# Cross-attention stage: inverse roots on POOL, unscaled exponentials, another order of PE's products

## The reference, cut to what matters

```python
x = x + attn(_layernorm(x), qkv_w, qkv_b, proj_w, proj_b)   # projection and residual end here
q = _layernorm(x)
kp = k @ Wk.T ; vp = v @ Wv.T + bv ; qp = q @ Wq.T + bq      # k = v = ctx, 77 rows a batch
scores = (qp @ kp.T) / sqrt(256)
x = x + (softmax(scores) @ vp) @ Wo.T + bo
xn = rmsnorm(_layernorm(x)) * norm_weight
logits = xn @ router_w.T + router_b ; probs = softmax(logits)
```

## Time and profile before

| what | us |
|---|---|
| median of three runs | 1166.14 (1165.2 to 1168.48) |
| profiled execution | 1170.64 |
| its span | 1168.9 |
| PE busy | 1066.8 (91%) |
| DVE busy | 1009.0 (86%) |
| ACT busy | 767.8 (66%) |
| POOL busy | 533.4 (46%) |
| the stage, first projection to last gates | 772.84 to 895.67 |

### The profile page before, as it was taken

How to read it: one execution, slowest core, us unless ns; L and a number is a source line. 1 busy time by engine, 2 the same in 40 slices (tenths; PEclk the granted TensorE clock), 3 DMA queues, 4 the chain that set the end, 5 groups by cost and what they waited for, 6 DMA issues and landing times. The chain is left out here.

```text
span 1168.9 us, 23162 instructions
## 1 busy us (share of the span) xinstructions
PE 1066.8 (91%) x8508; PEld 593.9 (51%) x8508; DVE 1009.0 (86%) x2108; ACT 767.8 (66%) x932; POOL 533.4 (46%) x866
## 2 busy tenths in 40 slices
PE   7988899999999999999999999988883069999998
PEld 6875433333333333333333333357773048888897
DVE  8998999999999999999999999437998975666653
ACT  4551288888888888888888888944555024555653
POOL 2647945454545363545444523232200023766665
PEclk8998599999999999999999999989997559999999
DMA  6787743232322334242424220055522022554443
GB/s 236 260 250 216 173 80 80 49 74 50 77 56 63 62 64 70 46 78 50 84 39 85 48 54 16 21 153 175 191 84 95 0 87 70 145 144 115 113 113 36
DMA packets 90140, 114.03 MB, mean 98 GB/s; under 512 B 31104, under 2 KB 62832, under 8 KB 90032
## 3 DMA queue, kind: packets, MB, share of 16 engines
q1 hardware_dynamic: 66872, 69.57, 20.5%
q0 software_dynamic: 19824, 36.48, 15.8%
q10 hardware_dynamic: 3336, 6.56, 1.6%
HBM read 73.31 MB, written 38.27 MB: 95 GB/s over the span
## 5 line engine op out<-in xcount | busy, mean ns | idle before, releaser
L835 DVE TENSOR_REDUCE b_max_halves<-banks 128x1 f32<-128x512 f32 x1024 | 625.1, 681 | 7.5 <-PE banks L882 7.5
L760 ACT ACTIVATE b_probs<-banks 128x1024 f32<-128x1024 f32 x512 | 520.4, 1027 | 110.8 <-PE banks L913 110.8
L882 PE MATMUL banks<-b_k,b_q 62*128 62x512 f32 x1024 | 391.9, 467 | 12.3 <-DVE b_max_halves L835 4.5
L913 PE MATMUL banks<-b_q,b_k 64*128 64x512 f32 x1024 | 378.8, 453 | 0.1
L898 PE MATMUL banks<-b_probs,b_v 128*17 128x256 f32 (+1 forms) x3840 | 314.3, 400 | 0.2 <-ACT b_probs L760 0.2
L913 PEld LDWEIGHTS banks<-b_q,b_k 64*128 64x128 f32 x1024 | 158.2, 185 | 228.6 <-issue 180.6
L882 PEld LDWEIGHTS banks<-b_k,b_q 62*128 62x128 f32 x1024 | 164.0, 189 | 38.3 <-DVE b_max_halves L835 33.6
L898 PEld LDWEIGHTS banks<-b_probs,b_v 128*17 128x17 f32 x3840 | 63.9, 95 | 164.8 <-issue 96.9
L572 POOL TENSOR_TENSOR b_att<-b_out,b_rec_spread 128x512 f32<-128x512 f32 x32 | 40.8, 1276 | 165.6 <-DMA b_rec_spread<-reciprocals 127.3
L1613 POOL DMA_INDIRECT e_x<-rows,d_idx x32 | 45.3, 1416 | 110.3 <-DVE d_wx L1788 56.8
L1833 DVE TENSOR_TENSOR e_hTl<-e_hT,e_hTh 128x512 fp32r<-128x512 f32 x64 | 47.8, 746 | 48.3 <-ACT e_hT L1587 48.3
(11 more groups left out here) (264 smaller groups left out, 1586.7 us busy)
## 6 DMA issues: line engine op xcount, KB each, us to landing
e_w<-in_w SPq DMA_DIRECT2D x16, 1024.0 KB, 7.6
q_stacks<-a_parts SPq DMA_DIRECT2D x32, 256.0 KB, 3.9
k_stacks<-a_parts SPq DMA_DIRECT2D x32, 256.0 KB, 4.2
b_q<-q_stacks POOLq DMA_DIRECT2D x60, 128.0 KB, 3.4
b_k<-k_stacks POOLq DMA_DIRECT2D x30, 256.0 KB, 4.9
v_tiles<-a_v ACTq DMA_DIRECT2D x8, 544.0 KB, 3.6
b_rec_spread<-reciprocals SPq DMA_DIRECT2D x128, 32.0 KB, 4.4
attended<-b_att SPq DMA_DIRECT2D x128, 32.0 KB, 2.4
```

Source lines behind the costliest of these rows:

```text
L760: nc.scalar.activation(pr[:, S % NP, u], ps[:, 2 * u:2 * u + 2, :], ACT.Exp, scale=D ** -0.5).then_inc(s_ex[u], 1)
L835: v.tensor_reduce(mxp[:, (k // NB) % 2, s, p, t, kh:kh + 1], ps[:, bank(k), :], AX.X, ALU.max)\
L882: nc.tensor.matmul(ps[:, bank(k), :], qs[g][stack, h, p, P * t:P * t + P], ks[g][stack, p, CH * kh:CH * kh + CH], start=True, stop=True).t ...
L913: return nc.tensor.matmul(ps[:, 2 * u + s, :], ks[g][stack, u, P * kt:P * kt + P], qs[g][stack, h, u, :], start=True, stop=True)
```

## The change

1. The inverse roots and `nm` leave DVE. POOL computes them for each step in `roots(s)`: 15 instructions, each waiting for the one before. Its guess is one instruction. POOL's order becomes: two biases, the scaling of the last attention block, then for each step its roots and the bias of chunk s+2.
2. The exponentials are transposed as they are. DVE only sums and inverts (`sums`), in the step after, ahead of the context product, and `attended` adds that product times the inverse sum to x1, in four instructions, one a tile.
3. The `vw` product is then unscaled too; `logits` scales it with one instruction more. `logits` and `gates` move from the start of steps 8 and 9 to behind the maxima.
4. PE's step becomes: `vo` and `vw` products of chunk s-2, all transposes of chunk s-1, one projection tile of chunk s+1, scores of chunk s-1, the other three tiles, idle products, transposes of the exponentials of chunk s-1.
5. ACT copies `pT` before it normalises, and the logit exponentials stand behind the softmax ones.

```diff
             for s in range(NS + 1):
-                if 0 <= s - 1 < J:
-                    act.wait_ge(s_st, s)
-                    normalise(xn[:, j % 2], x1[:, j % 3], j, 0, s_na)
                 if 0 <= s - 2 < J:
                     act.wait_ge(s_tp, s - 1)
                     copy(pT[:], ps[0:SK, 2, :]).then_inc(s_tpe, 1)
+                if 0 <= s - 1 < J:
+                    act.wait_ge(s_st, ROOT_STEPS * s)
+                    normalise(xn[:, j % 2], x1[:, j % 3], j, 0, s_na)
...
+            def attended(j, a, o):
+                for t in range(NT):
+                    if t % 2 == 0:
+                        dve.wait_ge(s_m2, 2 * j + t // 2 + 1)
+                    ins = v.scalar_tensor_tensor(o[:, t, :], ps[:, (3, 7)[t // 2], C * (t % 2):C * (t % 2) + C],
+                                                 rc[:, j, t:t + 1], a[:, t, :], ALU.mult, ALU.add)
...
-            def probabilities(j):
+            def sums(j):
                 x = j % 2
                 dve.wait_ge(s_ex, j + 1)
                 chain(v.tensor_reduce(sm[:, x], pe_[:, x], AX.X, ALU.add))
-                chain(v.reciprocal(rc[:, x], sm[:, x]))
-                v.tensor_tensor(pn[:, x], pe_[:, x], rc[:, x].unsqueeze(2).to_broadcast([P, NT, SK]),
-                                ALU.mult).then_inc(s_pn, 1)
+                chain(v.reciprocal(rc[:, j], sm[:, x]))
...
                 if second:
                     j = s - 2
+                    sums(j)
-                    residual(s_m2, s_m2e, j, (3, 7), x1[:, j % 3], x2[:, j % 2])
+                    attended(j, x1[:, j % 3], x2[:, j % 2])
...
-                guess(v, chain, *root)
-                newton(v, chain, *root)
+                variances_at.append(chain.n)
...
-                newton(v, chain, *root)
-                newton(v, chain, *root)
-                v.scalar_tensor_tensor(nm[:, s, u], mv[:, s, u, 0], -1.0, rs[:, s, u], ALU.mult, ALU.mult)\
-                    .then_inc(s_st, 1)
-                if 0 <= s - 1 < J:
-                    probabilities(s - 1)
+                if s == J:
+                    dve.wait_ge(s_st, ROOT_STEPS * J)
+                    logits(0, J - 2)
+                if s == J + 1:
+                    dve.wait_ge(s_st, ROOT_STEPS * (J + 1))
+                    logits(J - 2, J - 1)
+                    dve.wait_ge(s_gp, 1)
+                    gates(0, J - 2)
...
             tail.scale(pool, g, LAST, 1, NG * B)
+            step = Chain(pool, s_st, 0)
+            def roots(s):
+                u = slice(0 if s < J else NT, 2 * NT if s > 1 else NT)
+                pool.wait_ge(s_ch, variances_at[s])
+                y, a, t = rs[:, s, u], ve[:, s, u], tm[:, u]
+                step(g.tensor_scalar(y.bitcast(I32), a.bitcast(I32), -0.5, MAGIC, ALU.mult, ALU.add))
+                for _ in range(3):
+                    step(g.tensor_tensor(t, y, y, ALU.mult))
+                    step(g.tensor_tensor(t, t, a, ALU.mult))
+                    step(g.tensor_scalar(t, t, -0.5, 1.5, ALU.mult, ALU.add))
+                    step(g.tensor_tensor(y, y, t, ALU.mult))
+                step(g.tensor_scalar(t, mv[:, s, u, 0], -1.0, 0.0, ALU.mult, ALU.add))
+                step(g.tensor_tensor(nm[:, s, u], t, y, ALU.mult))
+            for s in range(NS):
+                roots(s)
+                if s + 2 < J:
+                    bias(s + 2)
...
+            def exponentials(j):
+                after(pe, s_tpe, j)
+                idle_products(7 if j >= J - 2 else 4 if j == 0 else 1)
+                pe.wait_ge(s_ex, j + 1)
+                for t in range(NT):
+                    last = mm(ps[0:SK, 2, P * t:P * t + P], pe_[:, j % 2, t, :], ident[:],
+                              is_transpose=True, start=True, stop=True)
+                last.then_inc(s_tp, 1)
+            for s in range(NS):
+                if s > 1:
+                    values(s - 2)
+                if 0 < s <= J:
+                    transposes(s - 1)
+                if s + 1 < J:
+                    project(s + 1, (0,))
+                if 0 < s <= J:
+                    scores(s - 1)
                 if s == 1:
                     fold_values()
                     pe.wait_ge(s_voe, 3)
                 if s + 1 < J:
-                    project(s + 1)
+                    project(s + 1, (1, 2, 3))
+                if 0 < s <= J:
+                    exponentials(s - 1)
```

More of the change, by code:

```diff
@@ L1150, in _ @@
                     last.then_inc(s_ex, 1)
[L1152 to L1167, removed]
+                if s == J:
+                    gate_exp(1, 0, J - 2)
+                if s == J + 1:
+                    gate_exp(2, J - 2, J - 1)
+                if s == NS:
+                    gate_exp(3, J - 1, J)
         @block.vector
@@ L1241, in _ @@
                 first, second = s < J, 0 <= s - 2
[L1242 to L1247, removed]
                 if first:
                     dve.wait_ge(s_xb, s + 1)
-                    residual(s_m1, s_m1e, s, (4, 5), xb[:, s % 2], x1[:, s % 3])
+                    residual(s, xb[:, s % 2], x1[:, s % 3])
                     ins = moments(0, x1[:, s % 3])
@@ L1292, in _, with bias @@
             gates(J - 2, J)
+        @block.gpsimd
+        def _(pool):
+            g = nc.gpsimd
+            g.memset(ones[:], 1.0).then_inc(s_one, 1)
+            pool.wait_ge(s_w, 10 * 16)
+            def bias(j):
+                pool.wait_ge(s_xi[j % 2], 16 * (j // 2) + 16)
+                after(pool, s_m1e, 2 * j - 2)
+                g.tensor_tensor(xb[:, j % 2], xs[:, j % 2], bp[:].unsqueeze(1).to_broadcast([P, NT, C]), ALU.add)\
+                    .then_inc(s_xb, 1)
+            bias(0)
+            bias(1)
+            tail.scale(pool, g, LAST, 1, NG * B)
+            step = Chain(pool, s_st, 0)
[15 more added lines that the diff above has]
+                    bias(s + 2)
         @block.tensor
@@ L1301, in product, with project @@
                 return last
-            def project(j):
+            def project(j, tiles=range(NT)):
                 q = j % 2
                 pe.wait_ge(s_at[q], 16 * (j // 2) + 16)
-                for t in range(NT):
+                for t in tiles:
                     if t % 2 == 0:
@@ L1352, in idle_products, with values, transposes @@
                     mm(ps[:, 2, 0:C], wp[:, 0, 0:P], wp[:, 0, :], start=True, stop=True)
[L1354 to L1358, removed]
-                    for t in range(NT):
-                        last = mm(ps[0:SK, 2, P * t:P * t + P], pn[:, s % 2, t, :], ident[:],
-                                  is_transpose=True, start=True, stop=True)
-                    last.then_inc(s_tp, 1)
-                at = lambda t: SZ * t
-                def transposes(j, k):
+            at = lambda t: SZ * t
+            def values(j):
+                pe.wait_ge(s_tpe, j + 1)
+                for t in range(NT):
+                    if t % 2 == 0:
+                        after(pe, s_m2e, 2 * j - 1 + t // 2)
+                    last = product(ps[:, (3, 7)[t // 2], C * (t % 2):C * (t % 2) + C],
+                                   [(pT[:, P * t:P * t + P], vo[:, j // 2, :])])
+                    if t % 2:
+                        last.then_inc(s_m2, 1)
+                pe.wait_ge(s_sce, j + 1)
+                for t in range(NT):
+                    last = product(ps[:, 6, at(t) + SW:at(t) + SZ], [(pT[:, P * t:P * t + P], vw[:, j // 2, :])])
+                if j == J - 1:
+                    last.then_inc(s_sc, 1)
+            def transposes(j):
+                pe.wait_ge(s_na, j + 1)
+                if j == 0:
+                    pe.wait_ge(s_kqe, KC + 1)
+                after(pe, s_tne, j)
+                for k in range(KC):
                     for t in range(NT):
@@ L1387, in _ @@
[L1387 to L1403 removed]
+                last.then_inc(s_tn, 1)
@@ new lines, in scores @@
+            def scores(j):
+                pe.wait_ge(s_tne, j + 1)
+                after(pe, s_sce, j)
+                for t in range(NT):
+                    last = product(ps[:, 6, at(t):at(t) + SW],
+                                   [(xnT[:, k, P * t:P * t + P], kqw[:, j // 2, k, :]) for k in range(KC)])
+                last.then_inc(s_sc, 1)
+            def exponentials(j):
+                after(pe, s_tpe, j)
+                idle_products(7 if j >= J - 2 else 4 if j == 0 else 1)
+                pe.wait_ge(s_ex, j + 1)
+                for t in range(NT):
+                    last = mm(ps[0:SK, 2, P * t:P * t + P], pe_[:, j % 2, t, :], ident[:],
+                              is_transpose=True, start=True, stop=True)
+                last.then_inc(s_tp, 1)
```

71 lines of the change are left out of this document (18 added, 53 removed).

## The result

| | us |
|---|---|
| changed, median of 4 runs | 1184.97 (1183.53 to 1189.45) |
| before, median of the 4 beside them | 1167.31 |
| ratio | 1.0154, 95% interval 1.0137 to 1.0172 |
| profiled execution of the changed kernel, its span | 1185.23, 1183.4 |

The forecast was 1169.4 with a range up to 1174.5. The change costs 17.7 us, five times the +3.3 of the sum.

What follows compares the result with a forecast made beforehand. DVE was taken as full now (11.12 us a step), PE's and ACT's chain as the bound after (11.1). Start +3.8, steps -1.9, end -0.7 and +2.1 made +3.3 on 1166.14: 1169.4 us, range 1164 to 1174.5.

Steps and rivals of the forecast that it cites:

- the +3.3 of the sum: Whole kernel: start +3.8, six steps -1.9, regained at the end -0.7, last roots +2.1, together +3.3 us.
- The steady step: Scores to scores in the middle steps: set by PE's and ACT's chain at 11.1 us, bounds 10.6 to 11.4.
- DVE idle before the scores: Sign of being right: in each step DVE idles about 2 us before PE's scores.
- rival E: Steady steps: chain less serial, DVE leads at 8.7, round under 9.9 us, whole 1155 us; chance 0.13.
- POOL's roots: Each step and the end: 15 dependent instructions take 4.4 us, between 3.0 and 5.3, hidden in the steps.
- The price of the early tile: Start: project(2)'s tile waits for its load until 794.9; scores of chunk 0 3.4 late, of chunk 1 +3.8 us.
- Rival C: POOL sets the step's pace or the end, +3 there from sharing with DVE, whole 1171 to 1175 us; chance 0.06.
- The 1.02 at 845.33: DVE's variance instruction, read as taking 1.02 us because it stops while POOL adds a bias.
- 1.7 for 1.28: DVE's context product with a scale: four half-width instructions, 1.7 us, for two that took 1.28; entered as +0.3.
- Rival B: Start: TensorE's clock falls in the new wait for the load, costing 1.5 to 3.5, whole 1171 to 1173 us; chance 0.22.
- From there as before: Behind the last roots, DVE's logits and first gates in their shadow: the remainder was taken as unchanged.
- A mis-sized term: the end: From the last scores to the gates: roots on POOL +2.1 us, 0.7 regained before them; last values 6.3 behind scores.

Runs made afterwards that it cites:

- e12: The changed kernel with idle products in PE's waits of step 1, in steps 7 and 8, and behind the exponentials' transposes in every step; 1176.94 us, ratio 1.0082.
- e8: e7 with five-chunk logits in DVE's slack of step 8, the vw product behind the row transposes, the early tile behind the exponentials' transposes; 1159.77 us, ratio 0.9935.
- e4: The changed kernel with ACT's first logit exponential moved behind the copy to pT of the last chunk; 1183.86 us, ratio 1.0125.
- e1: The changed kernel with the first tile of project(2) back behind the scores of chunk 0, in step 1 only; 1180.02 us, ratio 1.0116.
- e7: The changed kernel with e1, e2 and e4 together and the roots of steps 0 and 9 back on DVE; 1170.98 us, ratio 1.0036.
- e2: The changed kernel with two idle products in steps 7 and 8 in place of the missing projection tile; 1182.63 us, ratio 1.0129.
- e6: The changed kernel with idle products round the row transposes of step 1, three ahead and four behind; 1181.09 us, ratio 1.0108.
- e5: The kernel before, with POOL given one tiny memset behind the last roots at the stage's end; 1174.10 us, ratio 1.0061.
- e3: The changed kernel with the roots of step 9, the last, back on DVE; 1179.83 us, ratio 1.0117.
- e11: e7 with one idle product behind the transposes of the exponentials in every step, where PE waits for pT; 1169.45 us, ratio 1.0005.
- e10: e8 with idle products where PE works lightly, in step 2 and steps 6 to 8; 1163.26 us, ratio 0.9950.

## Why the prediction was wrong

It gave slower 0.48 and no change 0.39. The direction of its sum was right, the size was not.

**Right.** The steady step: 11.1 forecast, 11.08 in every undisturbed step. Without falls six steps save 2.0 (66.49 for 68.47, e12), 1.9 forecast. DVE idle before the scores, about 2 forecast, 1.67 measured. The round of PE and ACT is the chain, so rival E had no ground: its condition was a round under 9.9, and even e8's better order came to 10.0 to 10.15. POOL's roots: 4.4 forecast, 4.17 in a step (861.61 to 865.78) and 4.26 at the end (899.24 to 903.50); they stay hidden in the steps. The price of the early tile: +3.8 forecast at the start, +3.74 in e12 without the clock's part (40.66 for 36.92), and of it +3.4 forecast and +3.42 measured at the scores of chunk 0. Rival C was the term of DVE and POOL sharing at the end, +3; it measured 0.1. The Trainium skill ("GPSIMD Engine Reference", "Specifications") lets the two engines contend when DVE has two SBUF inputs; the trace agrees in direction, 4.26 beside DVE's logits for 4.15 at the start (785.69 to 789.84, the same 15 instructions), and the size is of no account here.

Three readings are slightly off, and nothing hangs on them. DVE's step has a wait of 0.16 ahead of the context sum, where the text says none. The 1.02 at 845.33 are two instructions, the longer of 0.95, and the same pair took 0.23 in the next step. And 1.7 for 1.28 adds 0.4 to DVE's step, not 0.3.

**The failed step: the clock.** Rival B had it as one fall at the start, 1.5 to 3.5, with 0.22. The fall came and cost 2.15 in the changed kernel's profile and 5.0 in e4's, but the mechanism is wider than the rival. PE's new order has a wait of 0.68 between transposes and values in every step, and 1.17 ahead of the scores where no tile follows. Falls came behind these waits too, the shorter ones over the row transposes, in other steps from run to run (step 2 in e1 and e7, steps 4 to 8 in e2, e4, e6 and the changed kernel). Altogether 8.4 us, from e12. That a wait costs its length was the tacit premise of the sum; here it cost more. The length of a wait alone isn't the sign: before, PE waited up to 1.02 us for DVE's probabilities, and its profile has no fall in the steps. Why the clock falls behind some waits and not behind others stays open.

**A missing term: the hand-over.** The end was summed up to the last gates, then "From there as before". That POOL is now the engine to end late, and takes 7.3 us to its next stage, cost 3.9 (e5, e3). POOL's 49.69 us of idle time before, put down to its own queue, don't say how much of it was needed, but the drain record in the same trace does: 6.9 us behind the last addition.

**A mis-sized term: the end.** +1.4 forecast (roots 2.1 less 0.7 regained), 2.7 measured. The 1.3 are the start of the last values, 7.57 behind their scores where the prediction had 6.3. They wait for the copy to `pT` of chunk 7, behind a logit exponential that waits for DVE's logits (2.06 for 0.68, e4). Part 5 of the change put it there; I read it as an order without cost.

Together 3.3 + 1.3 + 3.9 + 8.4 = 16.9, against 17.7 measured. The 3.3 is the forecast, not a measurement; with 1.3 and 3.9 it makes 8.5, inside e12's 7.7 to 11.6.

With all repairs nothing is won either: the stage of e11 is 123.73 for 123.11, six steps 2.0 shorter, start and end 0.3 and 2.3 longer.

## What to carry to other kernels

Work moved to an idle engine costs nothing only while nobody waits for its result sooner than the slower engine gives it, and while it doesn't make that engine the last one to leave the stage. After reordering PE's work, list each wait and what stands beside it: products that write nothing, put into them, were worth 0.72% in the changed kernel (e12), and in e10 nothing that can be told from e8. And where DVE is relieved, first look at the round of PE and ACT: here the gain came only when that order was changed as well (e8, e10). No run has the new order without the moved roots, or the unscaled exponentials alone.

## What the runs showed of the hardware

POOL took 7.1 to 7.3 us from its last instruction of this stage to its first of the next, after a memset of 0.10 us (e5) as after the roots, and 6.85 to 6.98 of it is a drain record of its queue; in e3, where POOL's last instruction lay 17 us ahead of the next stage, it cost nothing. At this stage's own start the same gap was 2.29 in the kernel before (770.36 to 772.65), so it isn't one figure for all stages. TensorE's clock fell at places that differ between executions of one order: step 7 of the changed kernel fell to the 1.2 GHz level within 870 to 880, and in e1, which has the same order there, it didn't. One profile tells where falls can come, and only several timed runs what they cost.
